# An attention kernel of two layers on one core: zero products ahead of the first operands, late PSUM claims, last stage by batch, and a new order of its steps

## The reference

```python
# layer 0: queries x, keys and values the context, causal (so only its first 112 tokens count)
Q = relu(x @ Wq.T + bq); K = relu(ctx @ Wk.T + bk); V = relu(ctx @ Wv.T + bv)
attn = softmax(where(tril, Q_ @ K_.T / sqrt(d), NEG)) * query_mask
x = layer_norm(merge(attn @ V_) + x) * gamma + beta
# layer 1: self-attention, cross-attention, feed-forward
q, k, v = split(layernorm(x, ln1) @ sa_wqkv)
result = x + merge(softmax(causal(q @ k.T * scale)) @ v) @ sa_wproj + sa_bproj
k2, v2 = split(layernorm(ctx, ln2) @ ed_wkv); q2 = layernorm(result, ln2) @ ed_wq
result = result + merge(softmax(q2 @ k2.T * scale) @ v2) @ ed_wproj + ed_bproj
result = result + relu(layernorm(x, ln3) @ ff_w1 + ff_b1) @ ff_w2 + ff_b2
```

## Time and profile before

| | us |
|---|---|
| median of 3 runs | 385.3 (382.94 to 386.32) |
| the profiled execution | 384.1 |
| its span, first to last instruction | 382.3 |
| TensorE busy in it | 341.8 |
| VectorE busy | 226.6 |
| ScalarE busy | 172.5 |
| GpSimd busy | 53.2 |

### The profile page before, as it was taken

The page is one execution under the profiler, slowest core; times in us unless marked ns, Lnnn a source line. Parts: engine busy times, 40 slices in busy tenths (PEclk is TensorE's granted clock), DMA queues, the critical chain, the costliest instruction groups (busy, mean ns, idle before and its releaser), DMA issues.

```text
span 382.3 us, 9700 instructions
## 1 busy us (share of the span) xinstructions
PE 341.8 (89%) x4144; PEld 261.7 (68%) x4144; DVE 226.6 (59%) x558; ACT 172.5 (45%) x297; POOL 53.2 (14%) x67
## 2 busy tenths in 40 slices
PE   7888699998999999998999999879989989887894
PEld 4666589886867777766668777655968757575663
DVE  5398997746657639564487545838943263645212
ACT  3346654465570263914326144655464535211551
POOL 2014141041320010120211012240100211000000
PEclk9999989999999999999999999999999999999999
DMA  7684103000000100000000020000000000000001
GB/s 223 186 328 137 63 2 104 3 2 2 25 2 0 45 40 24 3 2 2 24 6 3 0 82 2 3 0 26 3 2 2 2 2 2 3 0 0 3 2 48
DMA packets 4260, 13.43 MB, mean 35 GB/s; under 512 B 525, under 2 KB 1669, under 8 KB 3962
## 3 DMA queue, kind: packets, MB, share of 16 engines
q1 hardware_dynamic: 3928, 12.72, 10.0%
q10 hardware_dynamic: 290, 0.10, 0.1%
HBM read 11.89 MB, written 0.92 MB: 34 GB/s over the span
## 4 chain that ended last, share of the span: by engine, by line
PE 69%; DVE 16%; ACT 8%; issue 6%; ACTq 0%; DVEq 0%
PE ring L493 34%; PE ring L740 7%; DVE negmax L1021 7%; ACT exps L848 6%; PE ring L754 4%; PE ring L619 4%; PE ring L599 4%; PE ring L593 3%; PE acc L644 3%; PE ring L631 3%; DVE negmax L1000 3%; PE ring L663 2%; PE ring L611 1%; PE ring L705 1%; PE ring L525 1%
## 5 line engine op out<-in xcount | busy, mean ns | idle before, releaser
L1021 DVE TENSOR_REDUCE negmax<-ring 112x2 f32<-112x750 f32 x64 | 57.1, 936 | 42.2 <-PE ring L740 42.1
L848 ACT ACTIVATE exps<-ring 125x896 f32<-125x896 f32 x48 | 41.4, 914 | 43.7 <-PE ring L754 43.5
L1232 POOL TENSOR_SCALAR_AFFINE_SELECT exps<-exps 112x896 f32<-112x896 f32 x32 | 31.4, 1007 | 130.9 <-ACT exps L848 130.9
L1000 DVE TENSOR_REDUCE negmax<-ring 112x8 f32<-112x896 f32 x32 | 33.4, 1086 | 17.9 <-PE ring L599 17.7
L644 PE MATMUL acc<-exps,v 125*17 125x112 f32 (+1 forms) x1280 | 39.4, 264 | 0.8 <-ACT v L825 0.4
L644 PEld LDWEIGHTS acc<-exps,v 125*17 125x17 f32 (+1 forms) x1280 | 28.7, 98 | 13.8 <-issue 10.2
L848 ACT ACTIVATE exps<-ring,pad 112x896 f32<-112x896 f32 x32 | 30.5, 1004 | 16.7 <-PE ring L631 16.7
L740 PE MATMUL ring<-k,q 32*112 32x376 f32 x256 | 28.8, 517 | 10.2 <-DVE negmax L1021 6.0
L493 PE MATMUL ring<-w_b,h 128*112 128x256 f32 x128 | 29.5, 383 | 0.0
L619 PE MATMUL ring<-maxrows,sel 32*125 32x224 f32 (+1 forms) x320 | 19.1, 310 | 10.8 <-issue 2.9
L882 ACT ACTIVATE h<-ring,flat_c 128x224 f32<-128x224 f32 x32 | 11.7, 449 | 34.4 <-PE ring L493 34.4
(11 more groups left out here) (143 smaller groups left out, 552.1 us busy)
## 6 DMA issues: line engine op xcount, KB each, us to landing
c_nat<-in_ctx SPq DMA_DIRECT2D x4, 750.0 KB
w_b<-in_w_b SPq DMA_DIRECT2D x1, 2304.0 KB, 10.2
xk_t<-in_xk_t SPq DMA_DIRECT2D x4, 448.0 KB, 4.1
w_a<-in_w_a SPq DMA_DIRECT2D x1, 1280.0 KB, 5.7
xh<-in_keys SPq DMA_DIRECT2D x4, 224.0 KB, 2.8
x_nat<-in_x SPq DMA_DIRECT2D x4, 224.0 KB, 4.0
out<-x SPq DMA_DIRECT2D x4, 224.0 KB, 2.4
w_qk<-in_w_qk SPq DMA_DIRECT2D x1, 512.0 KB, 4.7
```

Source lines behind the costliest of these rows:

```text
L848: return nc.scalar.activation(exps[0:k, EXP_AT[job], :, :], o[0:k, :, 0:4 * T], ACT.Exp, bias=bias)
L1000: v_max[b].step(nc.vector.tensor_reduce(negmax[0][:, slot(g, b), 2 * m_:2 * m_ + 2, :], o[0:T, :, 0:4 * T].rearrange("p r (j t) -> p r j t ...
L1021: x_max[b].step(nc.vector.tensor_reduce(negmax[1][:, b, 2 * m_:2 * m_ + 2, i], o[0:T, :, 0:S], AX.X, ALU.max, negate=True), g, 2 * i + m_ + 1)
L1232: p_masked[b].step(nc.gpsimd.affine_select(e, e, [[0, 8], [1, T]], ALU.is_ge, 0.0, base=0, channel_multiplier=-1), g, k)
```

## The change

1. A memset of `idle` (256 columns of acc_sb in f32) is VectorE's first instruction, and ahead of its first step TensorE multiplies it by itself ten times as bf16, into a bank of ring 2 that later work overwrites.
2. xk_t and w_qk0 come in two halves each: queries and their weights, then keys and theirs, with a semaphore for each. q0 waits for the first, k0 for the second.
3. `quad` claims a pair only when its first bank is written.
4. S waits only for the masks of its own batch, the counts only for the fifth mask step.
5. The last stage is cut by batch: t2, y, the add and the store each exist once per batch, in streams B and F; t2 and y take a single bank each.
6. MIX is another string.

```diff
-            def store(g):
-                sp.wait_ge(*v_res.done(g))
-                sp.dma_start(out_d[g * G:(g + 1) * G, :, :].rearrange("b t f -> t b f"), x1[g % 2][:, :, :]).then_inc(stored[g % 2], 16)
+            def store(g, b):
+                sp.wait_ge(*v_res[b].done(g))
+                sp.dma_start(out_d[g * G + b, :, :], x1[g % 2][:, b, :]).then_inc(stored[g % 2], 16)
+            for part in range(2):
+                load_x(0, part)
+                sp.dma_start(w_qk0[:, part, :, :].rearrange("p c u -> p (c u)"), w_d["qk0"][:, part * C * U:(part + 1) * C * U]).then_inc((q0_loaded, k0_loaded)[part], 16)
-                pe.wait_ge(*v_mask.done(g))
+                pe.wait_ge(*v_mask.at(g, 5))
             def quad(step):
-                pair = [claim(pe, step + (m,)) for m in range(2)]
-                return [pair[r // 2][:, r % 2, :] for r in range(R)]
+                pairs = {}
+                def bank(r):
+                    if r // 2 not in pairs:
+                        pairs[r // 2] = claim(pe, step + (r // 2,))
+                    return pairs[r // 2][:, r % 2, :]
+                return bank
             def self_scores(g, l, b):
                 if l == 0:
-                    pe.wait_ge(*v_mask.done(g))
+                    pe.wait_ge(*v_mask.at(g, 7 + 2 * b))
-            def out2_transposed(g):
-                rows_transposed(("t2", g), o_nat[1], lambda b: pe.wait_ge(*x_o[b].done(g)))
+            def out2_transposed(g, b):
+                o = claim(pe, ("t2", g, b))
+                pe.wait_ge(*x_o[b].done(g))
+                for c in range(C):
+                    m = nc.tensor.transpose(o[:, 0, c * T:(c + 1) * T], o_nat[1][:, b, c * 128:(c + 1) * 128], ident[0:T, 0:T])
+                end(m)
-            def project_y(g):
-                pe.wait_ge(*a_ot[1].done(g))
-                tokens_out(("y", g), lambda b: token_pairs(o_t[1], b, wf["wp2"]))
+            def project_y(g, b):
+                o = claim(pe, ("y", g, b))
+                pe.wait_ge(*a_ot2[b].done(g))
+                end(products(token_pairs(o_t[1], b, wf["wp2"]), o[0:T, 0, 0:U]))
+            def keep_busy(n):
+                for _ in range(n):
+                    nc.tensor.matmul(ring[2][:, 1, :], idle.bitcast(BF16)[:, 0:128], idle.bitcast(BF16), start=True, stop=True, skip_group_check=True)
+            pe.wait_ge(prep_dve, 1)
+            keep_busy(10)
-            def result(g):
-                o = is_filled(dve, ("y", g))
-                for b in range(G):
-                    dve.wait_ge(*v_f[b].done(g))
-                v_res.step(nc.vector.tensor_tensor(x1[g % 2][:, :, :], o[0:T, :, 0:U], x1[g % 2][:, :, :], ALU.add), g, 1)
+            def result(g, b):
+                o = is_filled(dve, ("y", g, b))
+                dve.wait_ge(*v_f[b].done(g))
+                v_res[b].step(nc.vector.tensor_tensor(x1[g % 2][:, b, :], o[0:T, 0, 0:U], x1[g % 2][:, b, :], ALU.add), g, 1)
-MIX = ("RRLAANLNCNEDECDNCPAJCWNCWDEPIWDJINDPIJCIPDCDPIAJPAAIAJHJCJIHDEPCDPCEPEDCIDCDPJEAJIPAJAHAPINAAFIFJBPIJBKBABEPCHBNEBABPFBF"
+MIX = ("RARLALNNDNECAECDNCPJWCNCWDPIEWJICPDDCJPIDNDJPJAIPAAJAIDIHCHDCPJIEPCEEDCIDJCDHAHJPIPAJAKAINAPAEBIBJNBIJABEPBENBPBBBEFBFEB"
```

More of the change, by code:

```diff
@@ L103, in b_steps @@
 def b_steps(g, b):
-    return [("cS", g, b, i) for i in range(4)] + [("cM", g, b), ("cX", g, b, 0), ("cX", g, b, 1), ("cV", g, b, 0), ("cX", g, b, 2), ("cV", g, b, 1), ("cV", g, b, 2), ("cO", g, b)]
+    return [("cS", g, b, i) for i in range(4)] + [("cM", g, b), ("cX", g, b, 0), ("cX", g, b, 1), ("cV", g, b, 0), ("cX", g, b, 2), ("cV", g, b, 1), ("cV", g, b, 2), ("cO", g, b), ("t2", g, b), ("y", g, b)]
 GROUPS = range(NG)
@@ L148 @@
 NUMBER = {job: i for i, job in enumerate(JOBS)}
-SMALL = ("counts", "M", "O", "cM", "cO", "f")
+SMALL = ("counts", "M", "O", "cM", "cO", "f", "t2", "y")
 def homes():
@@ L293, in build @@
         y = v_tmp = keys_nat = xh
+        idle = acc_sb[2][:, :, :].rearrange("p s t -> p (s t)")[:, 0:256]
         unsplit = k2[1][:, :, :, :].rearrange("p b c s -> p (b c s)")[:, 0:C * 2 * U].rearrange("p (c u) -> p c u", c=C)
@@ L355, in build @@
         v_ctx = signal("ctx_steps", 2 * G * NCH + 1); v_cnm = signal("ctx_shift", 1); v_ct = signal("ctx_lo", G); v_v2 = signal("values2", G)
-        v_res = signal("result", 1)
+        v_res = each("result", 1)
         p_sd = each("deviation", 2, twin); p_rstd2 = twin("rstd2", G)
@@ L618, in minus_max @@
                         rows = slice(32 * r, 32 * r + 32)
-                        nc.tensor.matmul(bank[r][0:k, 2 * c * T:2 * (c + 1) * T], sel[rows, c:c + 1].to_broadcast([32, k]), maxrows[i][rows, :], start=c == 0, stop=False, skip_group_check=True)
+                        nc.tensor.matmul(bank(r)[0:k, 2 * c * T:2 * (c + 1) * T], sel[rows, c:c + 1].to_broadcast([32, k]), maxrows[i][rows, :], start=c == 0, stop=False, skip_group_check=True)
             def self_max_rows(g, l, b):
@@ L630, in self_shifted @@
                         rows = slice(32 * r, 32 * r + 32)
-                        m = nc.tensor.matmul(bank[r][0:T, 2 * c * T:2 * (c + 1) * T], kf[g % 2][rows, c, b, :],
+                        m = nc.tensor.matmul(bank(r)[0:T, 2 * c * T:2 * (c + 1) * T], kf[g % 2][rows, c, b, :],
                                              qf[g % 2][rows, c, b, :, :].rearrange("p e t -> p (e t)"), start=False, stop=True, skip_group_check=True)
@@ L683, in project_out1 @@
                 weights_in(g, wa_loaded)
-                pe.wait_ge(*a_ot[0].done(g))
+                pe.wait_ge(*a_ot1.done(g))
                 tokens_out(("proj", g), lambda b: token_pairs(o_t[0], b, wf["wp1"]))
@@ L739, in cross_scores @@
                     rows = slice(32 * r, 32 * r + 32)
-                    m = nc.tensor.matmul(bank[r][0:T, 0:SP], q2[g % 2][rows, c, b, e, :], k2[g % 2][rows, b, c, :], start=True, stop=True)
+                    m = nc.tensor.matmul(bank(r)[0:T, 0:SP], q2[g % 2][rows, c, b, e, :], k2[g % 2][rows, b, c, :], start=True, stop=True)
                     if r % 2:
```

81 lines of the change are left out of this document (45 added, 36 removed).

## The result

The changed kernel takes 373.07 us (370.09 to 373.21, 4 runs), the kernel before 385.77 (382.94 to 386.32) beside it: 0.967 of its time, interval 0.960 to 0.974. It is 12.7 us faster; I had forecast 5.6. The direction was right and the size was not: 373.07 lies inside the range, but in the rival that I gave 0.17 (and 371, where the range starts, is that rival's lower end, not its middle).

The account below looks back on a forecast made before the run. TensorE was taken as the bound (busy 341.8 of 382.3 us), so only its 40.5 idle us and low-clock stretches could be won. Terms -1.3 -0.8 -1.5 -2.5 +0.5 +0 = -5.6 gave 379.7 us; range 371 to 386.5.

Parts of the forecast that it names:

- the rival that I gave 0.17: Middle of the kernel: late claims let other steps follow each other, -8 to -14, so 371 to 377 us; chance 0.17.
- Pairs claimed late: Quads of scores: half of a quad runs before its second pair is claimed, shortening waits mainly at L740; -1.5 (0 to -4).
- for X and cX 2 of 16, nothing: Shifted scores: only 2 of 16 matmuls come before the second claim, so late claims gain nothing there.
- Split, the second half needs some 0.7 again: L740 quads: a wait w costs w+0.7 and not w+0.9, saving 0.15 to 0.2 at each of 22 waits.
- The slower rival: L740: split quads lose their strips' overlap, 1.20 and not 0.90 for each of 32; +5.5, 390.8 us; chance 0.10.
- The new merge: The new step order otherwise, in the middle: no sum found, 0 (-8 to +5); quads following within 1.1 us 29, now 35.
- The start: Zero products raise TensorE's clock at 6.1 us, S starts at 13.4, not 14.67: -1.3; +1.9 if it rises as late as before.
- The slow stretch at 47 us: Low clock from 47 to 51 us loses 1.7; the order puts V 0 0 1 there; half taken, -0.8.
- The end by batch: Last stage: halved y, t2, copy and add save 2.35, the smaller store's landing 0.15; -2.5.
- The moved work: y of pair 2 and half of t2 move ahead of the last exponentials, 3/4 hidden in waits: +0.5 (0 to +2.2).
- Halves of the first loads: Start: the first loads in halves cost nothing, SP issuing its halves 0.9 us later, under the zeros.
- My sign for being wrong on the whole: TensorE's idle time between 20 and 360 us moving by more than 4 us either way.

Follow-up runs that it names:

- e1: The kernel before with late claims alone, a quad claiming each PSUM pair when first written: 375.14 us, 0.972 of the kernel before.
- e9: The kernel before with late claims in the cross scores alone, both pairs claimed first in S, X and cX: 379.52 us, 0.985.
- e12: e8 with the 16 matmuls of X and cX regrouped, all of the first pair's ahead of the second claim: 375.90 us, 0.975 of the kernel before.
- e4: The changed kernel with the steps in the old order, the last stage's steps by batch at their old place: 374.94 us, 0.971 of the kernel before.
- e2: The changed kernel with early claims, quads claiming both pairs first: 390.99 us over ten runs, 390.34 over seven, 1.010 of the kernel before.
- e5: The changed kernel with the flag ahead of rows 1, rows 1 behind the second S, keys ahead of general: 373.02 us, 0.967 of the kernel before.
- e6: The changed kernel with both groups' rows first, as in the kernel before, zeros kept: 370.28 us, 0.964 of the kernel before.
- e7: The kernel before with the last stage (t2, y, add, store) by batch alone, at the old places: 384.70 us, 0.999.
- e8: The changed kernel with the start of e5 and without the ten zero products: 369.52 us, 0.964 of the kernel before.

## Why the prediction was right or wrong

- **Pairs claimed late, -1.5: this term was mis-sized**, and it is the error of the whole; alone it measured -10.3. Three steps of it failed. (a) "for X and cX 2 of 16, nothing": they gave 2.4 us alone. TensorE waited 10.8 us ahead of their quads, as long as ahead of L740, and I did not look that row up. (b) "Split, the second half needs some 0.7 again", so that "a wait w then costs w+0.7": the second half takes 0.89, a wait costs w+0.9 as before, and at that line nothing was gained in the changed kernel (39.0 and 39.0; in e1 it is 36.1). The term counted TensorE alone; what it left out is the reader, whose first maximum waits only for the first half: VectorE's wait for the cross scores fell by 8.5 us in e9. (c) "those at 0.2 us give little": they were priced one by one, but a pair that is read earlier is free earlier for the next quad. That this is how the time adds up is likely and not shown.
- **The slower rival: wrong in mechanism, and its price came out near by luck.** The cross scores' busy time rose by 8.9 us, 0.28 us for each of 32 quads, and I had 0.30. But the strips are not kept apart in every quad: the 12 that meet no wait take 0.90, and the 8.9 us are waits that now lie inside the quads, as waits and work are 39.0 us before and after. Where a regrouping does keep the strips apart without a wait, as in e12, a quad loses 0.3 us.
- **The new merge, 0: right as far as can be told.** The order as a whole is -1.9 with late claims and some +4 with early ones (e4, e2), but the start and the end, which are terms of their own here, are in it; without them nothing clear of noise is left with late claims. The counts of quads that follow each other closely (29, now 35) did point at the dependence on the claims, and I drew no number from it.
- **The start, -1.3: wrong sign.** S starts at 16.00, not at 14.67. No run shows the -1.3, for a rise at 6.1 us, nor the +1.9, for one at 12.8: the changed kernel was profiled with a rise at 10.5 alone, and S came 1.3 us later and not earlier. Zeros took 4.45 us (I had 4.3), the q half landed at 4.3. That keys behind general would hold the masks was right (ksum at 13.88). The step that failed is the time of the rise: I took 6.1 us, it was 10.5, though e4, e5 and e6 show that the early case exists too (5.7, 5.7 and 4.3). I had not foreseen a fall after it, from 13.9 to 20.7. What decides when the clock rises or falls is not shown: in e6 it rose at 4.3 us among the zeros, in the changed kernel only at 10.5 behind the same ones, and the seven falls behind one-row products came with TensorE busy for 3.4 to 4.0 of the 4 us ahead.
- **The slow stretch at 47 us, -0.8:** it went (1.7 us), but the kernel got the longer one at the start for it. e1 in the old order still is free of it from 46 to 52 and has one between 20 and 30 us (0.83), so its place goes with small shifts and not with V 0 0 1.
- **The end by batch, -2.5: right.** From the last exponential to the end of the last add it is 5.4 us and not 7.5, and the landing 1.8 and not 2.4, more than the 0.15 that I took. By e7 and e4 the cut gives 0.6 of the 2.1 us and the landing, the new places the other 1.5.
- **The moved work, +0.5:** not measured by itself. e4 and e1 have the same time, though e4 has zeros (with the rows first 0 to +1.7) and the cut: the cut with y of group 2 still at the end can't have given much.
- **Halves of the first loads:** free, as said; q0's operands came at 4.3 us, but the zeros kept TensorE until 5.6, so they gave nothing either.
- **My sign for being wrong on the whole came true:** TensorE's idle time between 20 and 360 us went from 31.0 to 11.4, by 19.5 us and not under 4, though part of that now counts as work at the cross scores' line.

## What to carry to other kernels

Claim a buffer where it is first written, not where a group of writes begins. Here a parted group kept its writer as long as before; what came earlier is the start of its reader. So price such a change on the reader too, and look up every line that waits ahead of the same helper: adding up the writer's waits one by one gave 1.5 us where 10.3 were to be had. An order made for one rule of claiming can be worse than the old one under the other, so test them together. And products put in to bring an engine's clock up have to be out of the way when the operands land: here they helped in none of three starts.

## What the runs showed of the hardware

Four matmuls on four 32-row strips take 0.90 us where each record lasts 0.52; parted by a wait, the last two take 0.89 by themselves (changed kernel, 133.97). At two strips at a time, the 16 matmuls of X and cX take 1.56 us and not 1.24 in a quad (e12, e8). TensorE's clock rose at 4.3 to 5.7 us, among or behind the zeros, in three profiles and at 10.3 and 10.5 in two with the same first instructions. It fell from 1.00 to 0.50 behind one-row products in seven profiles, with TensorE busy for 3.4 to 4.0 of the 4 us ahead, and stayed there for 6.8 us in four of them and 3.4 in three; in e8, with the start of e12, one of the seven, it did not fall. A store of 112 KB landed in 1.8 us, one of 224 KB in 2.4.
